# The first group's feed-forward layer in one pair of banks, eight early panels and result gathers in two bursts

## The chip, the cores and the metric

One core of a Trainium2 chip runs the whole program in one launch. The metric is the device time of one execution in microseconds (us). The engines are TensorE (PE, matrix products; its weight loads are shown apart as PEld), VectorE (DVE), ScalarE (ACT), GpSimd (POOL) and SyncE (SP). Each has an instruction stream of its own that runs in order; the streams meet by semaphores. SP and POOL issue nearly all transfers.

## The reference

Two layers over 2 sequences of 1024 tokens with 256 features, a context of 64 rows each:

```
x = x + tanh(g_xattn[0]) * attention(layernorm(x), ctx)       # one head, 64 keys
x = x + tanh(g_ffn[0])   * moe(layernorm(x))                  # 16 experts, 2 per token, + its input
x = x + tanh(g_xattn[1]) * (layernorm(x) @ W1.T + mean(ctx) @ W2.T + b)
x = x + tanh(g_ffn[1])   * ffn(layernorm(x))
moe(h): top 2 of softmax(h @ gate); y = sum_e comb_e * (silu(h @ w1_e) * (h @ w3_e)) @ w2_e
ffn(h): h = silu(h @ w1) * (h @ w2)        # 256 -> 1024, weights -1, 0, 1 with a scale per column
        h = gelu(h @ h1); h = gelu(h @ h2) # 1024 -> 1024 each
        h @ w3                             # 1024 -> 256
```

## The kernel before, in words

The 2048 tokens are 16 tiles of 128 rows and four groups of four tiles (512 tokens). Products run in fp32r, so every operand is split into a high and a low part; an expert product is three matmuls (low times high, high times low, high times high), and a product of the last layer two, since its weights are exact in the high part.

**Stage 1** (to about 65 us) is attention, routing and the expert weights' split. Tokens are sorted by expert into 47 blocks of 128 rows (`NBLK`): the first 16 blocks are the first 128 rows of each expert, the rest follow.

**Stage 2** is the loop over expert blocks, `for i in range(NBLK + DOWN)`, on each engine. POOL gathers the rows of block i (`L659`) up to six blocks ahead (`NXG`). PE turns block i + 2 (`turns`, `L1850`), together with the hidden rows of block i - 2 (`L1853`; this matmul is the mark of a turn below: the mark of block n is the turn made in iteration n - 2), runs `gate_up(i)` and then `down(i - 4)`. ACT copies the turned rows out as the high part (`high_turned`), applies silu and copies results out (`rows_out`); DVE makes the low part (`low`) and the product with the gate. SP stores the results to `ys_dram`. The results that the first group's tokens need are all in the first 16 blocks' part of `ys_dram` once those are stored, so the first group's next steps are woven into this loop at hand-written iteration numbers (`Y_AT` to `LOW4_AT`): POOL gathers the eight result tiles (`gather_rows`, `L640`), DVE adds them (`row_added`), and then, in halves of two tiles, come the statistics, the root on POOL (`root_half`, `L588`), the transposes (`turned_half`, `L1896`), high and low parts, the product with W1 (`part1_half`), the row that POOL adds (`add_row_half`, `L648`), and the same again for the LayerNorm ahead of the last layer. Iteration numbers on POOL count row gathers, which run ahead of PE's.

**Stage 3** is the feed-forward network for the four groups (`ffn(g)`), 512 tokens at a time: a first layer of eight chunks m (eight matmuls of 128 x 512 each, gate and up in one pair of banks, `L2007`, `L2010`), two layers h1 and h2 of eight chunks (16 matmuls each, `L2038`, `L2039`), and the product with w3. In the first layer, chunk m writes the pair `bank[2 * (m % 2)]` and the next, so two pairs alternate; ACT applies silu (`L1573`), DVE multiplies with the up half (`L1296`), ACT rounds the high part (`L1577`), DVE makes the low part (`L1300`).

The last layer's weights are 44 panels of 128 x 512 (`NPAN`): 0 to 7 the first layer, 8 to 23 h1, 24 to 39 h2, 40 to 43 w3. SP loads them (`load_raw`, `L375`), at most four in flight, and they are rounded in place: 0 to 7 by DVE, the others by ACT (`round_panels`, `L1531`), which counts them in `act_pan`. Panels 0 to 15 are loaded during the expert loop, 16 to 21 when the last result is stored, 22 to 43 when the first layer of the first group is through (`f_pe[FK - 1]`). What sets these times is the memory: the panels' places are used by expert weights and by the first group's buffers until then. ACT rounds five panels in the last iterations of the loop, nine in the first group's first layer and the rest in h1.

Of the kernel before, what the change touches and what calls it, by code (L numbers as in the profile page):

```python
# [25 lines left out]
ALU = mybir.AluOpType  # L26
# [25 lines left out]
NRAW = 16  # L52
# [6 lines left out]
FIRST_PAN = NRAW + (3 * 4 * 4 * 256) // (4 * 512)  # L59
# [56 lines left out]
def flamingo_kernel(nc, x, ctxT, cols, rows, wq, wkT, wvT, gate, experts, w1T, w2T, panels, consts, identity, out):  # L116
    with ExitStack() as ctx:
# [19 lines left out]
        Wr, w_end = place("Wr", [P, NPAN * PANEL], F32R)  # L137
        w_off = w_end - 4 * NPAN * PANEL
        Wraw = nc.alloc_sbuf_tensor_at("Wraw", [P, NPAN * PANEL], F32, offset=w_off)
        Ah, _ = place("Ah", [P, 4096], F32R)  # L140
        Al, _ = place("Al", [P, 4096], F32R)
        Bh, _ = place("Bh", [P, 4096], F32R)
        bl_off = at[0]
        Bl, b_end = place("Bl", [P, 4096], F32R)
# [55 lines left out]
        e_off = w_end - 4 * LATE * PANEL  # L200
# [73 lines left out]
        put = over(w_off + 4 * NRAW * PANEL, e_off)  # L274
        y_first = [put(f"y_first{r}", [P, TG, D]) for r in range(TOPK)]
        xn_first = put("xn_first", [P, TG, D])
        xTh_first, xTl_first = put("xTh_first", [P, DK, GN], F32R), put("xTl_first", [P, DK, GN], F32R)
        yb = put("yb", [P, 4, D])
# [69 lines left out]
        bank_t, bank_gu = [bank[0], bank[1], bank[4]], [bank[2], bank[3]]  # L348

        bank_y, bank_first = [bank[6], bank[5]], bank[7]  # L350
# [20 lines left out]
        def load_raw(eng, w):  # L371

            if w >= 4:
                eng.wait_ge(dma_pan[w % 4], 16 * (w // 4))
            eng.dma_start(Wraw[:, w * PANEL:(w + 1) * PANEL], panels[w]).then_inc(dma_pan[w % 4], 16)  # L375
# [7 lines left out]
        def panel(w):  # L383
            return Wr[:, w * PANEL:(w + 1) * PANEL], Wraw[:, w * PANEL:(w + 1) * PANEL]
# [9 lines left out]
        def half_turned():  # L394
            return bank_first[:, :].rearrange("p (k n) -> p k n", k=DK)
# [14 lines left out]
        def _(eng):  # L410
# [62 lines left out]
            panel_at = [PAN_AT + 3 * (w // 2) + w % 2 if w < DVE_PAN else PAN_AT + 12 + 2 * (w - DVE_PAN) for w in range(NRAW)]  # L473
            for i in range(NBLK + 2):
# [3 lines left out]
                if i == PAN_AT:  # L478
# [3 lines left out]
                    eng.wait_ge(pool_el, EL_CUT * POOL_EL)  # L482
                    eng.wait_ge(dve_el, E - POOL_EL)
                    eng.wait_ge(act_setup, ACT_LATE + 2)
                    for b in range(2):
                        eng.wait_ge(dma_xb[b], 16 * rows_stored[b])
# [54 lines left out]
        def _(eng):  # L541
# [108 lines left out]
            for i in range(NBLK):  # L650
# [13 lines left out]
                if i == Y_AT[0]:  # L664
# [11 lines left out]
                    eng.wait_ge(dve_el, E - POOL_EL)  # L676
                    for b in range(2):
                        eng.wait_ge(dma_xb[b], 16 * rows_stored[b])
                if i in Y_AT:
# [1487 lines left out]
```

## Time and profile before

| | us |
|---|---|
| timed runs | 494.70, 500.42, 785.72 |
| median of them | 500.42 |
| span of the profiled execution, first to last instruction | 514.8 |
| PE busy in it | 482.9 |
| DVE, ACT, POOL busy | 317.2, 214.0, 147.2 |

The profile is one execution, and not one of the timed runs; its own time outside the span is not listed. A busy PE is an engine with a matmul under way; matmuls overlap, so the distance between two starts tells more than the duration of one. "Idle before" in a row names what ended the wait.

### The profile page before, as it was taken

The page shows a single profiled execution, that of the slowest core. Times are in us where ns is not written, and L with a number is a line of the kernel's source. Part 1 is how long each engine was busy: PE and PEld are TensorE (multiplying, and loading weights), DVE is VectorE, ACT ScalarE, POOL GpSimd, SP SyncE. Part 2 cuts the span into 40 slices and gives each one's busy share as a digit, 9 for nine tenths or more (in the row PEclk, how much of TensorE's full clock was granted, in tenths as well). Part 3 has the DMA queues.
Part 4 walks back from the last instruction along what each step waited for, and adds up shares of the span by engine and source line. Part 5 has one row for each costly group of instructions (what it writes and reads, how often), then busy time and mean ns, then how long its engine had stood idle before and what let it go on. Part 6 is the DMA issues. An engine that isn't in the chain of part 4 may idle for free.

```text
span 514.8 us, 7849 instructions
## 1 busy us (share of the span) xinstructions
PE 482.9 (94%) x2754; PEld 414.0 (80%) x2754; DVE 317.2 (62%) x850; ACT 214.0 (42%) x444; POOL 147.2 (29%) x154
## 2 busy tenths in 40 slices
PE   8898977994889899999999999999999999999996
PEld 7787867893879678888987888897888888788886
DVE  3988855872668577548456874537677633745433
ACT  4569924671547695621254221126222133621210
POOL 1677674647562141101071110126011101000000
PEclk9989997997799999999999999999999999999999
DMA  8967432795572558422041220005032002021101
GB/s 290 339 251 245 156 93 83 211 290 167 166 220 94 177 185 268 148 81 61 22 143 43 64 78 24 1 1 163 22 102 62 1 1 81 2 77 66 42 1 47
DMA packets 34480, 58.81 MB, mean 114 GB/s; under 512 B 4545, under 2 KB 18369, under 8 KB 34370
## 3 DMA queue, kind: packets, MB, share of 16 engines
q1 hardware_dynamic: 29776, 47.12, 27.9%
q0 software_dynamic: 3840, 10.49, 7.2%
q10 hardware_dynamic: 818, 0.61, 0.4%
q8 instruction: 25, 0.41, 0.3%
q14 instruction: 21, 0.17, 0.1%
HBM read 47.85 MB, written 14.42 MB: 121 GB/s over the span
## 4 chain that ended last, share of the span: by engine, by line
PE 77%; DVE 4%; another core or an unknown queue 3%; ACT 2%; issue 2%; DMA 1%; POOLq 0%
PE bank L2038 23%; PE bank L2039 23%; PE bank L2010 6%; PE bank L2007 5%; PE bank L1613 3%; PE bank L1615 3%; PE bank L1614 3%; PE bank L2071 3%; PE bank L2070 3%; PE bank L1850 2%; PE bank L1853 1%; DVE turned L1019 1%; ACT xb L1429 1%; DMA xg_more<-xb_dram,perm 1%
## 5 line engine op out<-in xcount | busy, mean ns | idle before, releaser
L1587 ACT ACTIVATE sg<-bank,colv 128x512 f32<-128x512 f32 x64 | 44.1, 690 | 177.2 <-PE bank L2039 177.2
L2038 PE MATMUL bank<-Ah,Wr 128*128 128x512 f32 x256 | 100.3, 392 | 0.6 <-DVE sg L1296 0.6
L2038 PE MATMUL bank<-Bh,Wr 128*128 128x512 f32 x256 | 99.9, 390 | 0.0
L2039 PE MATMUL bank<-Bl,Wr 128*128 128x512 f32 x256 | 99.7, 389 | 0.0
L2039 PE MATMUL bank<-Al,Wr 128*128 128x512 f32 x256 | 99.7, 389 | 0.0
L2038 PEld LDWEIGHTS bank<-Ah,Wr 128*128 128x128 f32 x256 | 48.0, 188 | 11.9 <-DVE sg L1296 1.4
L2039 PEld LDWEIGHTS bank<-Bl,Wr 128*128 128x128 f32 x256 | 48.1, 188 | 9.8
L2038 PEld LDWEIGHTS bank<-Bh,Wr 128*128 128x128 f32 x256 | 48.1, 188 | 9.8
L2039 PEld LDWEIGHTS bank<-Al,Wr 128*128 128x128 f32 x256 | 48.1, 188 | 9.7
L1313 DVE CAST Ah<-sg 128x512 fp32r<-128x512 f32 x32 | 13.6, 426 | 60.1 <-ACT sg L1587 60.1
L1613 PE MATMUL bank<-EL,turned 128*128 (+1 forms) x133 | 42.7, 321 | 1.2 <-issue 0.9
L583 POOL TENSOR_TENSOR rstd<-veps,mhalf 128x4 f32<-128x4 f32 x6 | 8.4, 1400 | 108.8 <-DVE veps L762 61.1
L1614 PE MATMUL bank<-EH,turned 128*128 (+1 forms) x133 | 38.7, 291 | 0.0
L1615 PE MATMUL bank<-EH,turned 128*128 (+1 forms) x133 | 38.5, 290 | 0.0
L1296 DVE SCALAR_TENSOR_TENSOR sg<-bank,colv,sg 128x512 f32<-128x512 f32 x32 | 24.0, 751 | 23.1 <-ACT sg L1573 20.3
L1573 ACT ACTIVATE sg<-bank,colv 128x512 f32<-128x512 f32 x32 | 22.1, 690 | 38.4 <-PE bank L2010 35.3
L1313 DVE CAST Bh<-sg 128x512 fp32r<-128x512 f32 x32 | 13.6, 426 | 39.4 <-ACT sg L1587 39.4
L2007 PE MATMUL bank<-xTh,Wr 128*128 128x512 f32 x96 | 37.7, 392 | 0.0
L2010 PE MATMUL bank<-xTl,Wr 128*128 128x512 f32 x96 | 37.6, 392 | 0.0
L659 POOL DMA_INDIRECT xg<-xb_dram,perm x32 | 31.7, 991 | 15.5 <-PE bank L1853 6.9
L1019 DVE TENSOR_TENSOR turned<-bank,turned 128x384 fp32r<-128x384 f32 (+1 forms) x47 | 24.9, 530 | 13.6 <-ACT turned L1505 7.7
L2071 PE MATMUL bank<-Wr,Al 128*128 128x256 f32 x128 | 30.9, 283 | 0.0
(295 smaller groups left out, 1036.9 us busy)
## 6 DMA issues: line engine op xcount, KB each, us to landing
Wraw<-panels SPq DMA_DIRECT2D x44, 256.0 KB
stage<-panels SPq DMA_DIRECT2D x44, 256.0 KB
ES<-experts SPq DMA_DIRECT2D x16, 384.0 KB, 5.7
ys_dram<-yb SPq DMA_DIRECT2D x47, 128.0 KB
ys_dram<-x SPq DMA_DIRECT2D x1, 1920.0 KB, 8.8
X<-x SPq DMA_DIRECT2D x3, 512.0 KB, 7.8
xb_dram<-xb SPq DMA_DIRECT2D x3, 512.0 KB, 4.5
out<-outb SPq DMA_DIRECT2D x3, 512.0 KB
```

Source lines behind the costliest of these rows:

```text
L659: eng.indirect_dma_start(out=rows, out_offset=None, in_=xb_dram, in_offset=bass.IndirectOffsetOnAxis(ap=perm[:, i:i + 1], axis=0)).then_in ...
L1019: eng.tensor_tensor(low_[:, w], bank_t[b][:, w], high_[:, w].bitcast(F32), ALU.subtract).then_inc(b_xl, 1)
L1313: own(eng.tensor_copy(h[0][:, m, :], sg[:, r, :]))
L1587: eng.activation(sg[:, (8 * layer + m) % 3, :], bank[m % 4][:, :], ACT.Gelu, scale=colv[:, c + m:c + m + 1]).then_inc(f_act[m], 1)
L1613: mm(dst, lhs[0], rhs[1], start=first, stop=False)
L1614: mm(dst, lhs[1], rhs[0], start=False, stop=False)
L1615: return mm(dst, lhs[0], rhs[0], start=False, stop=last)
L2007: mm(dst, w[:, u, k, :], x_high[:, k, :], start=k == 0, stop=False)
L2010: ins = mm(dst, w[:, u, k, :], x_low[:, k, :], start=False, stop=k == DK - 1 and not general)
L2038: mm(bank[m % 4][:, :], Wr[:, base:base + P], h[0][:, k, :], start=k == 0, stop=False)
L2039: ins = mm(bank[m % 4][:, :], Wr[:, base:base + P], h[1][:, k, :], start=False, stop=k == FK - 1 and not general)
L2071: ins = mm(dst, hA[1][:, k, j * P:(j + 1) * P], w, start=False, stop=k == FK - 1)
```

## The change

Memory: the hidden tensors A and B of stage 3, which had places of their own, become part of one array of 76 slots of 128 x 512 (`SLOTS`), and panels are mapped to slots by `slot(w)`. Only panels 0 to 7 are loaded in the loop (`NRAW = 8`); 8 to 39 follow as soon as the last expert block's product is done, 40 to 43 when the first layer of the first group is through.

Result gathers: on POOL four follow row gather 30 and four row gather 31. The counts of stored blocks are read by four register loads in place of one instruction for all four. The half steps lie closer together (iterations 27 to 36), and each half has a bank of its own (`bank_half`); therefore from block 30 on the turns use two banks instead of three.

First layer: for the first group it moves out of `ffn` into `first_chunk`, which can be woven into the loop by `CHUNK_AT`; here that list is empty, so all eight chunks follow the last iteration. Chunks 0 to 5 and 7 use `bank[7]` and `bank[4]`, chunk 6 `bank[5]` and `bank[6]`. ACT writes silu's result to `first_gate`. ACT rounds panels 8 and 9 ahead of chunk 7 and 10 and 11 behind it, three per chunk of h1, and one per chunk of h2.

```diff
-NRAW = 16
+NRAW = 8
-FIRST_PAN = NRAW + (3 * 4 * 4 * 256) // (4 * 512)
+SLOTS = NPAN + 4096 * 4 // PANEL
+HID_A = NRAW
-Y_AT = (28, 29, 31, 32, 34, 35, 37, 38)
-ROOT2_AT, ROW_AT, ROOT3_AT = (37, 45), (38, 45), (44, 46)
-ADD_AT, STAT_AT = (25, 28, 31, 36), (26, 29, 33, 37)
-TURN3_AT, HIGH3_AT, LOW3_AT, PART_AT, X3_AT = (30, 37), (31, 38), (32, 39), (33, 40), (34, 41)
-NORM_AT, TURN4_AT, HIGH4_AT, LOW4_AT = (43, 45), (44, 47), (45, 48), (46, 48)
+Y_AT = (30, 30, 30, 30, 31, 31, 31, 31)
+ROOT2_AT, ROW_AT, ROOT3_AT = (32, 33), (32, 34), (36, 38)
+ADD_AT = (27, 28, 29, 29)
+LOW3_AT, X3_AT, NORM_AT, LOW4_AT = (29, 30), (30, 32), (33, 35), (34, 36)
+TURN3_AT, PART_AT, TURN4_AT = (29, 30), (29, 31), (34, 36)
+HIGH3_AT, HIGH4_AT = (29, 30), (34, 36)
+CHUNK_AT = ()
+RING2 = 30
-RESIDUAL_AT = (12, 13, 14, 15, 27, 30, 38, 40, 44, 47)
+RESIDUAL_AT = (12, 13, 14, 15, 24, 25, 39, 41, 43, 45)
...
+        bank_half = [bank[7], bank[4]]
+        bank_first = [[bank[5], bank[6]] if m == FK - 2 else [bank[7], bank[4]] for m in range(FK)]
+        def bank_t(n):
+            return bank[n % 2] if n >= RING2 else (bank[0], bank[1], bank[4])[n % 3]
+        def slot(w):
+            return w if w < NRAW else w + NPAN - LATE - NRAW if w < NPAN - 4 else w - NPAN + 4 + HID_A + 16
...
-            eng.wait_ge(n_T4, 2)
-            for b in range(4):
-                eng.wait_ge(dma_ys[b], 16 * len(range(b, NBLK, 4)))
             eng.wait_ge(b_y, NBLK)
             for n in range(NRAW, NPAN):
-                if n == FIRST_PAN:
+                if n == NPAN - 4:
                     eng.wait_ge(f_pe[FK - 1], 1)
...
-                    _, stored_n = nc.values_load_multi_w_load_instructions(
-                        stored[0:1, 0:4], engines=(mybir.EngineType.Pool,), min_val=16 * (E // 4),
-                        max_val=16 * (NBLK // 4 + 1), skip_runtime_bounds_check_because="DVE counts the blocks")
+                    stored_n = [eng.value_load(stored[0:1, b:b + 1], min_val=16 * (E // 4), max_val=16 * (NBLK // 4 + 1)) for b in range(4)]
...
-                if i in Y_AT:
-                    gather_rows(0, [Y_AT.index(i)])
+                gather_rows(0, [n for n in range(TOPK * TG) if Y_AT[n] == i])
...
+            def first_up(m):
+                eng.wait_ge(f_act[m], 2)
+                eng.scalar_tensor_tensor(first_gate[:, m, :], bank_first[m][1][:, :], colv[:, C_S2 + m:C_S2 + m + 1],
+                                         first_gate[:, m, :], ALU.mult, ALU.mult).then_inc(f_h[m], 1)
+            def first_low_part(m):
+                eng.wait_ge(f_hh[m], 1)
+                eng.tensor_tensor(hA[1][:, m, :], first_gate[:, m, :], hA[0][:, m, :].bitcast(F32),
+                                  ALU.subtract).then_inc(f_hl[m], 1)
+            def first_chunk(m):
+                first_up(m)
+                if m > 0:
+                    first_low_part(m - 1)
+                if len(RESIDUAL_AT) + m < NT:
+                    residual(len(RESIDUAL_AT) + m)
...
+            def first_high_part(m):
+                eng.wait_ge(f_h[m], 1)
+                if m == FK - 2:
+                    for b in range(4):
+                        eng.wait_ge(dma_ys[b], 16 * len(range(b, NBLK, 4)))
+                eng.activation(hA[0][:, m, :], first_gate[:, m, :], ACT.Copy).then_inc(f_hh[m], 1)
+            def first_chunk(m):
+                eng.wait_ge(f_pe[m], 1)
+                eng.activation(first_gate[:, m, :], bank_first[m][0][:, :], ACT.Silu,
+                               scale=colv[:, C_S1 + m:C_S1 + m + 1]).then_inc(f_act[m], 1)
+                if m > 0:
+                    first_high_part(m - 1)
...
-                if NBLK - 5 <= i < NBLK:
-                    round_panels(1)
+            for m in range(len(CHUNK_AT), FK):
+                if m == FK - 1:
+                    round_panels(2)
+                first_chunk(m)
+            first_high_part(FK - 1)
+            round_panels(2)
...
-                        if g == 0 and layer == 1:
-                            round_panels(3 if m else 2)
+                        if g == 0:
+                            round_panels(3 if layer == 1 else 1)
...
                 if n >= 3:
-                    eng.wait_ge(b_xl, n - 2)
+                    eng.wait_ge(b_xl, n - 1 if n >= RING2 + 2 else n - 2)
...
+            def first_chunk(m):
+                if m == 0:
+                    eng.wait_ge(n_l4, 2)
+                elif m == FK - 2:
+                    eng.wait_ge(b_ye, NBLK)
+                else:
+                    eng.wait_ge(f_h[m - 1 if m < FK - 1 else m - 2], 1)
+                eng.wait_ge(dve_pan, m + 1)
+                w = panel(m)[0].rearrange("p (u k n) -> p u k n", u=2, k=DK)
+                for u in range(2):
+                    for k in range(DK):
+                        dst = bank_first[m][u][:, :]
+                        mm(dst, w[:, u, k, :], xTh_first[:, k, :], start=k == 0, stop=False)
+                        ins = mm(dst, w[:, u, k, :], xTl_first[:, k, :], start=False, stop=k == DK - 1)
+                ins.then_inc(f_pe[m], 1)
+            for m in range(len(CHUNK_AT), FK):
+                first_chunk(m)
```

## Rows read from the trace of the kernel before

**Rows 1.** The page: span, and busy time, share and instructions of each engine.
```profile
span 514.8 us, 7849 instructions
PE 482.9 (94%) x2754; PEld 414.0 (80%) x2754; DVE 317.2 (62%) x850; ACT 214.0 (42%) x444; POOL 147.2 (29%) x154
```

**Rows 2.** Timeline of PE: start us, us, engine, line, tiles, count [idle before <-releaser].
```profile
108.32 0.27 PE L1853 MATMUL bank<-ident,bh 128*128 128x128 f32 x1
109.73 0.27 PE L1853 MATMUL bank<-ident,bh 128*128 128x128 f32 x1
...
117.25 0.27 PE L1853 MATMUL bank<-ident,bh 128*128 128x128 f32 x1
...
136.06 0.29 PE L1853 MATMUL bank<-ident,bh 128*128 128x128 f32 x1
...
140.89 0.27 PE L1853 MATMUL bank<-ident,bh 128*128 128x128 f32 x1
...
166.62 0.27 PE L1853 MATMUL bank<-ident,bh 128*128 128x128 f32 x1
...
169.55 0.66 PE L1896 MATMUL bank<-ident,xn_first 128*128 128x128 f32 x4 [1.12 <-DVE xTl_first L1166]
...
172.42 0.50 PE L2007 MATMUL bank<-xTh_first,Wr 128*128 128x512 f32 x1 [0.47 <-ACT yb L1519]
```

**Rows 3.** The chain that ended last, in order of time: start us, us, what.
```profile
116.97 3.12 another core or an unknown queue
...
125.61 4.50 another core or an unknown queue
```

**Rows 4.** Timeline of POOL, 110 to 143 us.
```profile
110.19 0.95 POOL L659 DMA_INDIRECT xg<-xb_dram,perm  x1 [0.98 <-PE bank L1853]
114.41 0.95 POOL L640 DMA_INDIRECT y_first<-ys_dram,slots  x1 [3.27 <-DMA ys_dram<-yb]
115.66 0.94 POOL L659 DMA_INDIRECT xg_more<-xb_dram,perm  x1 [0.30 <-issue]
...
138.38 0.72 POOL L588 TENSOR_TENSOR rstd<-veps,mhalf 128x2 f32<-128x2 f32 x1 [1.95 <-DVE veps L1161]
...
141.58 1.30 POOL L648 TENSOR_TENSOR X<-X,crow 128x512 f32<-128x512 f32 x1
```

**Rows 5.** Line 668 alone: duration in ns (min/median/max), first and last start.
```profile
L668 POOLq TENSOR_LOAD <-stored x1: 520/520/520, 110.0 to 110.0; - x1
```

**Rows 6.** The chain in order of time, at the first row gather.
```profile
65.21 2.80 DMA xg_more<-xb_dram,perm
```

**Rows 7.** Timeline of PE: a turn that waited for its row gather.
```profile
119.72 0.41 PE L1850 MATMUL bank<-ident,xg_more 128*128 128x128 f32 x2 [1.08 <-DMA xg_more<-xb_dram,perm]
```

**Rows 8.** The chain in order of time: a half's transposes, one 256-wide matmul.
```profile
137.43 0.44 PE bank L1896 x4
...
138.19 0.12 PE bank L1613
```

**Rows 9.** Timelines of ACT, DVE and PE in the first feed-forward layer.
```profile
174.55 0.69 ACT L1573 ACTIVATE sg<-bank,colv 128x512 f32<-128x512 f32 x1 [2.18 <-PE bank L2010]
175.34 0.75 DVE L1296 SCALAR_TENSOR_TENSOR sg<-bank,colv,sg 128x512 f32<-128x512 f32 x1 [3.04 <-ACT sg L1573]
187.32 0.40 PE L2038 MATMUL bank<-Ah,Wr 128*128 128x512 f32 x1
```

**Rows 10.** Stretches: us, busy of PE, PEld, DVE, ACT, POOL, granted clock, DMA, GB/s.
```profile
118.00:122.00 4.00, 2.26 (x15) 1.59 (x13) 0.29 (x1) 0.66 (x2) 2.92 (x4) 1.00 0.58 189
...
130.00:136.00 6.00, 5.20 (x24) 5.19 (x25) 3.96 (x11) 2.92 (x9) 4.30 (x5) 0.50 0.63 175
...
168.00:172.00 4.00, 2.52 (x18) 1.91 (x16) 2.39 (x7) 3.22 (x12) 0.00 (x0) 1.00 0.32 107
```

**Rows 11.** Timeline of SP behind the first feed-forward layer.
```profile
187.51 19.59 SPq L375 DMA_DIRECT2D Wraw<-panels  x22
```

**Rows 12.** Groups of instructions by line: busy us, mean ns of one.
```profile
L1531 ACT ACTIVATE Wr<-Wraw 128x512 fp32r<-128x512 f32 x36 | 21.0, 623 | 0.0
```

More of the change, by code:

```diff
@@ L134, in sem, with hidden @@
             return ctx.enter_context(nc.semaphore(name))
[L137 to L144, printed above, removed]
+        Wr, w_end = place("Wr", [P, SLOTS * PANEL], F32R)
+        w_off = w_end - 4 * SLOTS * PANEL
+        Wraw = nc.alloc_sbuf_tensor_at("Wraw", [P, SLOTS * PANEL], F32, offset=w_off)
+        def hidden(name, slot):
+            return [nc.alloc_sbuf_tensor_at(f"{name}{part}", [P, 4096], dt, offset=w_off + 4 * PANEL * (slot + 8 * n))
+                    for n, (part, dt) in enumerate((("h", F32R), ("l", F32R)))]
+        Ah, Al = hidden("A", HID_A)
+        Bh, Bl = hidden("B", SLOTS - 16)
+        first_gate = nc.alloc_sbuf_tensor_at("first_gate", [P, FK, GN], F32, offset=w_off + 4 * PANEL * (HID_A + 8))
+        bl_off, b_end = w_off + 4 * PANEL * (SLOTS - 8), w_off + 4 * PANEL * SLOTS
         X, _ = place("X", [P, NT, D])
@@ L374, in load_raw @@
                 eng.wait_ge(dma_pan[w % 4], 16 * (w // 4))
-            eng.dma_start(Wraw[:, w * PANEL:(w + 1) * PANEL], panels[w]).then_inc(dma_pan[w % 4], 16)
+            eng.dma_start(panel(w)[1], panels[w]).then_inc(dma_pan[w % 4], 16)
         rows_stored = [NG // 2, NG // 2 - 1 + 2]
@@ L383, in panel @@
         def panel(w):
[L384 removed]
+            columns = slice(slot(w) * PANEL, (slot(w) + 1) * PANEL)
+            return Wr[:, columns], Wraw[:, columns]
         def counted(g):
@@ L471, in ys_blocks @@
                 return ys_dram.rearrange("(b p) d -> b p d", p=P)[i]
-            panel_at = [PAN_AT + 3 * (w // 2) + w % 2 if w < DVE_PAN else PAN_AT + 12 + 2 * (w - DVE_PAN) for w in range(NRAW)]
+            panel_at = [PAN_AT + 3 * (w // 2) + w % 2 for w in range(NRAW)]
             for i in range(NBLK + 2):
@@ L1239, in _ @@
                         low_half(q, n_h4, n_l4)
+                for q in range(2):
+                    for j in (2 * q, 2 * q + 1):
+                        if i == ADD_AT[j]:
+                            row_added(0, j)
+                            row_statistics(0, j)
+                            if j % 2:
+                                variance_half(2, q)
+                        if i == LOW3_AT[q] and j % 2 == q:
+                            low_half(q, n_h3, n_l3)
+                    if i == X3_AT[q]:
+                        x3_half(q)
+                        statistics3_half(q)
+                if i in CHUNK_AT:
+                    first_chunk(CHUNK_AT.index(i))
+            for m in range(len(CHUNK_AT), FK):
+                first_chunk(m)
+            first_low_part(FK - 1)
             own.done()
@@ L1292, in ffn @@
                 g3 = 3 * g
-                for m in range(FK + 1):
+                for m in range(FK + 1 if g else 0):
                     if m < FK:
@@ L1301, in ffn @@
                                           ALU.subtract).then_inc(f_hl[m - 1], 1)
-                    if g == 0 and len(RESIDUAL_AT) + m < NT:
-                        residual(len(RESIDUAL_AT) + m)
                 if g == 0:
@@ L1502, in high_turned @@
             def high_turned(n):
-                b, w = n % 3, joint(n)
+                w = joint(n)
                 eng.wait_ge(b_tx, n + 1)
-                eng.activation(turned_pair(n)[0][:, w], bank_t[b][:, w], ACT.Copy).then_inc(b_xh, 1)
+                eng.activation(turned_pair(n)[0][:, w], bank_t(n)[:, w], ACT.Copy).then_inc(b_xh, 1)
             def silu(i):
@@ L1559, in _ @@
                         high_half(q, n_T4, n_h4)
-                if NBLK - 5 <= i < NBLK:
-                    round_panels(1)
+                if i in CHUNK_AT:
+                    first_chunk(CHUNK_AT.index(i))
+            for m in range(len(CHUNK_AT), FK):
[4 more added lines that the diff above has]
+            round_panels(2)
             def ffn(g, more):
                 g3 = 3 * g
-                for m in range(FK + 1):
+                for m in range(FK + 1 if g else 0):
                     if m < FK:
@@ L1944, in _ @@
                     if i == TURN4_AT[q]:
-                        if q:
-                            eng.wait_ge(n_l4, q)
                         turned_half(q, xn_first, n_xn, n_T4)
+                if i in CHUNK_AT:
+                    first_chunk(CHUNK_AT.index(i))
+            for m in range(len(CHUNK_AT), FK):
+                first_chunk(m)
             def T3(g):
@@ L1987, in low_part @@
                     return Wlo[:, w % 2, :]
-                for m in range(FK):
+                for m in range(FK if g else 0):
                     if m >= 2:
@@ L2020, in ffn @@
                         if m < 4:
-                            if layer == 1:
+                            if layer == 1 and g:
                                 eng.wait_ge(f_h[6 + m // 2], g + 1)
-                            else:
+                            elif layer == 2:
                                 eng.wait_ge(f_act[m + 4], g3 + 2 + 1)
```

84 lines of the change are left out of this document (27 added, 57 removed).

## The prediction

> **What bounds the kernel now.** I read the page first, then the chain that ended last, then the timeline of TensorE (PE), POOL, ACT and DVE in the expert stage and in the first feed-forward layer. PE is busy 94% of a span of 514.8 us [rows 1], so a change counts by the PE time that it opens or closes. Two places are not bound by PE's own work. The expert blocks should run at one block per 1.41 us (from one turn mark to the next) [rows 2], but between the turns of block 28 and of block 32 four blocks took 18.81 us instead of 5.64 [rows 2]. The chain gives 12.2 us of that to "another core or an unknown queue", in four pieces of 3.12, 1.44, 3.12 and 4.50 [rows 3]. I call these 13.2 us the hole. At the loop's end PE waits for the second half of the first group's LayerNorm chain, 1.12 us ahead of its transposes, and 0.47 us for the last output copy [rows 2]. Behind the loop PE runs matmul after matmul.
>
> **Which time the sum is made against.** The profiled execution's own run time is not listed, only its span, 514.8. Without the hole that is 501.6; the median of the timed runs is 500.42, the lowest 494.7. So the timed runs hold little of the hole, and I make the sum on the trace without it and add the difference to 500.42.
>
> **The change, part by part.**
>
> *A. The result gathers in two bursts.* Before, eight gathers lie one by one between the row gathers 28 to 38; afterwards four follow row gather 30 and four follow 31. A gather takes POOL 1.25 us start to start, and row gather 28 started at 110.19 [rows 4], so 30 starts at 112.69 and ends at 113.64. The four block-count registers now take four loads; the one load before took 520 ns [rows 5]. Three more make 1.56, and the burst starts at 115.2 (bounds: 113.9 if the loads are hidden; 117 if the wait for stored blocks, 3.27 us before [rows 4], still ends last). Then row gather 31 starts at 115.2 + 4 x 1.25 = 120.2 and row gather 32 at 126.45. A row gather lands 2.80 us after its start where it is on the chain alone [rows 6]; the one that started at 115.66 held PE until 119.72, 4.06 us, with panel loads beside it [rows 4, 7]. I take 2.80, since no panel is loaded there any more, and keep 4.06 for the range. So block 32 can be turned at 129.3. At PE's pace it was due at 117.25 + 4 x 1.41 = 122.9 [rows 2]: 6.4 us late. DVE waits in the same stretch for gathers 4 to 7 ahead of adding rows 2 and 3, and behind it in DVE's queue stands the low half of block 32, which is not there yet either; so this costs nothing twice. The first half's transposes (0.44) and its 12 products (12 x 0.12 = 1.4) [rows 8] fall into PE's wait and are paid.
>
> Next POOL does the root (0.72) and the row add (1.30) [rows 4] ahead of row gather 33, which starts at 129.7 and lands at 132.5; PE would want it at 129.3 + 1.41 + 0.44 = 131.1, so another 1.4 late. Then 1.41 for the block and 1.4 for the second half's products: block 34 at 135.3. Row gather 35 stands behind the second root and add and lands at 137.0, 0.3 late. So block 35 is turned at 137.0. Before it was at 140.89, without the hole 127.7 [rows 2]. **A costs 9.3 us by then** (6 to 13 with the bounds above; three landings are on the path).
>
> *B. From block 35 to the first layer.* Before this took 172.42 - 140.89 = 31.5 us [rows 2], with one half's transposes, both products and the LayerNorm waits in it. Afterwards two sets of transposes are left (0.9), 13 turns at 1.41 make 18.3, and the tail after the mark of block 48 is before's 172.42 - 166.62 = 5.8 without the last transposes (a wait of 1.12, then 0.44) and without the 0.47 wait: 3.8 [rows 2, 8]. Sum 23.0, so **B gives back 8.5**. With only two turn banks from block 30 on, the turn of n waits for the low half of n-2 instead of n-3; PE's products for that block wait for it right behind, so I cost it at nothing. That holds while ACT and DVE keep up with 1.41; if they do not, each block pays the lag. ACT's five panel roundings leave the loop; ACT was not last there, so nothing.
>
> *C. The first layer.* Before, its 64 products run from 172.42 to 187.32 in two pairs of banks, 14.9 us, 1.86 a chunk [rows 2, 9]. Afterwards chunks 0 to 5 and 7 share one pair, and chunk m waits until DVE has read chunk m-1. From a chunk's first product to ACT's start is 2.13, ACT takes 0.69, DVE follows 0.10 later and takes 0.75 [rows 9], and I add 0.05 back to PE: 3.72 a chunk. Five of these, then chunk 5, chunk 6 (its own banks) and chunk 7 back to back, 3 x 1.86: 24.2 us. **C costs 9.3.** ACT's and DVE's other work per chunk (rounding the high part, the low part, a residual) fits into the 3.7. PE then stands still for nearly half of this stage. In this trace the clock fell after a stretch with 2.26 us busy of 4 and stayed at 0.50, the 1.2 GHz level, through 130 to 136, but stayed at 1.00 through one with 2.52 of 4 [rows 10]; a chunk would show about 2.0 of 3.7. I take the full clock, as the products are wide.
> The Trainium skill, "TensorE: Matmul & The Clock Gate" (A second HAM failure mode: psum-queue depth-cycling), has a kernel whose PE idles briefly between groups because its PSUM banks are cycled, and whose clock swings between both levels. By that rule this stage would be dearer than by the row; that is a rival below.
>
> *D. Panels.* 32 panels now load behind the last expert block and four behind the first layer. SP issued 22 in 19.59 us, 0.89 each [rows 11]; the first that counts is rounded 22 us later, and the second layer uses two in 16 x 0.233 = 3.7 us. No wait; cover: layer C itself. ACT rounds three per chunk in the second layer and one in the third, and the 36th comes after the third layer's last activation. PE waits there for all 36 ahead of the last product: 0.1 + 0.69 + 0.62 [rows 9, 12] = **1.4 us**, which before did not exist, as all were rounded a layer earlier. SP's queue loses the panels between result stores; nobody waits for those.
>
> **Sum:** 9.3 - 8.5 + 9.3 + 1.4 = +11.5, so 500.4 + 11.5 = 511.9 us, 2.3% slower. Own range of this case: 507 to 517 (A's bounds).
>
> **Rivals.**
> 1. *The hole is half in the timed runs and the panels make it (not slower).* The hole lies at blocks 26 to 30, and SP loads panels 8 to 15 from block 20 to 34, between result stores; those eight loads leave this place. For it: the runs spread by 5.7 us (494.7 to 500.42), and the row gather of this stretch landed 1.3 us later than the one alone [rows 6, 7]. Against it: result stores and gathers stay, now in bursts. If the median holds those 5.7 us and the change frees them, the result is 494.7 + 11.5 = 506.2, 1.2% above, the same within what is measurable. It decides once about 1.5 us of such time is in the usual run. Freeing 21 us, which a gain of 2% would need, is more than the whole hole.
> 2. *The clock falls in layer C.* At 1.2 GHz a chunk's products take twice 1.86. All eight chunks low: +14.9 us; one low stretch as long as the shorter ones of the trace, about half of that. Time 519, at most 527. For: the row with 2.26 of 4. Against: the row with 2.52 of 4, and that every product is 512 columns wide. It is the mechanism of the skill's rule named above; no run here shows it in such a stage.
> 3. *The bursts are cheaper.* If the four loads run ahead of the engine and PE reaches block 31 later than I have it, A falls to 6: 508.6, 1.6% over and so within what can be told apart.
>
> **How the numbers follow.** Forecast (511.9) 0.50; rival 1 0.24; rival 2 0.13; rival 3 0.08; something unseen, either way, 0.05. The prediction is the first. The range 502 to 520 reaches over rivals 1 and 3 and the cheaper half of 2. A measurement of this kernel tells about 2% from no change, here 510.4. Slower: 0.7 of the forecast, which lies close to that line, rival 2 and a little of the rest: 0.51. Faster: a rest of rival 1, 0.05. Within 2%: 0.44.
>
> **What would show it.** In the changed kernel's trace: on POOL two runs of four result gathers with a row gather between; PE idle ahead of the turn of block 32 for 4 us or more, released by a gather; six groups of eight 512-wide products about 3.7 us apart, PE waiting for DVE between them, and two more without a gap; about 1.4 us of idle PE, released by ACT, ahead of the last product's first matmul in the first group; a loop end with no wait on the LayerNorm chain. I am wrong if the loop ends much earlier than before at equal start (then the bursts cost little or the hole was the panels'), if chunks follow at 1.9 us, or if the clock drops behind the last block.

## The result, and the profile after

The changed kernel took 509.01 us (median of 4 runs, 507.82 to 510.97); its ratio to the kernel before is 1.0251, 95% interval [1.019, 1.0311]. Run once more later, as *changed_again*, it took 508.59 beside 494.77 of the kernel before (17 runs): 1.0243 [1.0198, 1.0288]. The ratios are worked out from fast runs alone, with executions more than 1.5% above the fastest of their kernel set aside (785.72 and 501.46 of the kernel before, 501.44 of late_panels below). They are not the quotients of the medians shown, which for changed_again would be 1.028. So the change costs 10 to 14 us. That it costs time is clear; that it costs 2% is not quite, since the intervals begin at 1.019 and 1.0198. The forecast was 511.9, range 502 to 520.

The page of the changed kernel, its span and busy times; they answer to [rows 1].

```profile
span 508.8 us, 7841 instructions
PE 478.7 (94%) x2754; PEld 411.7 (81%) x2754; DVE 317.7 (62%) x850; ACT 218.6 (43%) x444; POOL 147.0 (29%) x154
```

The span is 6 us *shorter* than that of [rows 1], though the kernel is slower. The two profiled executions are not alike, and the page alone would mislead. This run took 510.97 in all, 2.2 more than its span.

PE's timeline in the changed kernel answers to [rows 2], with the marks of turns on L1896 (blocks 28, 32, 35 and the last), the first layer on L1965, h1 on L2094 and w3 on L2126.

```profile
107.98 0.27 PE L1896 MATMUL bank<-ident,bh 128*128 128x128 f32 x1
...
115.00 0.66 PE L1893 MATMUL bank<-ident,xg 128*128 128x128 f32 x2 [2.87 <-DMA xg<-xb_dram,perm]
...
119.91 0.39 PE L1656 MATMUL bank<-W1l,xTh_first 128*128 128x256 f32 x1 [1.41 <-DVE xTl_first L1170]
...
121.67 0.27 PE L1896 MATMUL bank<-ident,bh 128*128 128x128 f32 x1
...
127.87 0.39 PE L1656 MATMUL bank<-W1l,xTh_first 128*128 128x256 f32 x1 [2.61 <-DVE xTl_first L1170]
...
132.56 0.27 PE L1896 MATMUL bank<-ident,bh 128*128 128x128 f32 x1
...
154.12 0.30 PE L1896 MATMUL bank<-ident,bh 128*128 128x128 f32 x1
...
156.10 0.40 PE L1965 MATMUL bank<-xTh_first,Wr 128*128 128x512 f32 x1
...
159.67 0.50 PE L1965 MATMUL bank<-xTh_first,Wr 128*128 128x512 f32 x1 [1.56 <-DVE first_gate L1199]
...
180.88 0.47 PE L2094 MATMUL bank<-Ah,Wr 128*128 128x512 f32 x1 [0.68 <-ACT Wr L1553]
...
245.25 0.36 PE L2126 MATMUL bank<-Wr,Ah 128*128 128x256 f32 x1 [1.34 <-issue]
```

Three things stand here. The loop waits in brackets: for the row gather of block 31 (2.87) and twice for a low half made by VectorE (1.41, 2.61). The first six chunks of the first layer follow 3.6 to 3.7 apart, each but the first behind a wait of 1.56. And 1.34 us of idle stand ahead of w3. The profile names no releaser for it ("issue"); the kernel has PE wait there for ACT's count of panels, and round_four below bears that out.

POOL's timeline in the changed kernel answers to [rows 4]: result gathers on L650, row gathers on L669, the root on L598.

```profile
106.30 0.95 POOL L650 DMA_INDIRECT y_first<-ys_dram,slots  x1 [2.07 <-DMA ys_dram<-yb]
...
111.38 0.95 POOL L669 DMA_INDIRECT xg<-xb_dram,perm  x1 [0.30 <-PE bank L1896]
...
117.64 0.94 POOL L669 DMA_INDIRECT xg<-xb_dram,perm  x1 [0.30 <-issue]
...
123.94 0.72 POOL L598 TENSOR_TENSOR rstd<-veps,mhalf 128x2 f32<-128x2 f32 x1 [2.17 <-DVE veps L1165]
124.86 1.02 POOL L669 DMA_INDIRECT xg<-xb_dram,perm  x1 [0.19 <-issue]
```

The two bursts are there, 5.0 us each. The first row gather behind a burst started at 111.38 and held PE until 115.00. In the chain its landing is 3.49 (the prediction had taken 2.80), while POOL shows only 0.95. The Trainium skill, "Perfetto Trace Analysis" (DMA Instruction — SWDGE (GPSIMD)), says that such an instruction's end is the end of descriptor generation and not of the data movement; this trace agrees. The row gather of block 34 (124.86) stands behind a root that waited 2.17 for VectorE.

Stretches of the changed kernel (columns as in [rows 10]): two in the loop, two in the first layer.

```profile
114.00:119.00 5.00, 3.50 (x16) 3.28 (x16) 2.08 (x6) 1.62 (x4) 4.06 (x5) 0.66 0.43 125
...
128.00:132.00 4.00, 4.00 (x22) 4.00 (x23) 0.93 (x3) 0.49 (x1) 3.18 (x5) 0.57 0.23 66
...
156.00:163.00 7.00, 4.24 (x19) 2.85 (x17) 1.51 (x3) 2.55 (x5) 1.90 (x2) 1.00 0.81 263
163.00:181.00 18.00, 12.26 (x49) 8.78 (x50) 9.29 (x17) 7.49 (x14) 5.07 (x5) 1.00 0.90 299
```

The clock fell in the loop, behind the gaps there, and not in the first layer.

**Where the time went, by stage.** The table has differences of start times in PE's timelines, in us, so scatter of the start drops out. The column "usual before" is *before_four_loads* (below), since [rows 2] turned out to be unusual.

| stage | usual before | changed | difference | forecast |
|---|---|---|---|---|
| mark of block 28 to mark of block 35 (A) | 15.47 | 24.58 | +9.11 | +9.3 |
| mark of block 35 to the first layer (B) | 30.59 | 23.54 | -7.05 | -8.5 |
| first layer to h1 (C) | 14.91 | 24.78 | +9.87 | +9.3 |
| h1 to the end of the span (D) | 326.38 | 327.92 | +1.54 | +1.4 |
| sum | | | +13.5 | +11.5 |

Each column is one profile, and A depends on which: the seven blocks took 21.93 in the profile of changed_again and 13.64 in that of late_panels, a kernel that has A as before, so A lies between 6.5 and 10.9. B and D differ by less than 0.5 between the two profiles of the changed kernel, C by 1.8.

### The profile page after: what moved, and what is told of

Same layout as the page of the kernel before. It is cut to its first block, busy times and chain, and to the rows that moved or that the text cites. A ratio compares the mean times of both kernels' runs of the same rounds, so it can differ in the third digit from the quotient of the medians.

```text
span 508.8 us, 7841 instructions
## 1 busy us (share of the span) xinstructions
PE 478.7 (94%) x2754; PEld 411.7 (81%) x2754; DVE 317.7 (62%) x850; ACT 218.6 (43%) x444; POOL 147.0 (29%) x154
## 4 chain that ended last, share of the span: by engine, by line
PE 77%; DVE 3%; DMA 3%; ACT 2%; POOL 1%; issue 1%; POOLq 0%
PE bank L2094 23%; PE bank L2095 23%; PE bank L2063 4%; PE bank L2066 4%; PE bank L1656 3%; PE bank L1657 3%; PE bank L1658 3%; PE bank L2126 3%; PE bank L2127 3%; PE bank L1893 2%; PE bank L1965 2%; DMA xg<-xb_dram,perm 1%; PE bank L1966 1%; PE bank L1896 1%; ACT first_gate L1577 1%
## 5 line engine op out<-in xcount | busy, mean ns | idle before, releaser
L1630 ACT ACTIVATE sg<-bank,colv 128x512 f32<-128x512 f32 x64 | 44.1, 690 | 172.0 <-PE bank L2095 172.0
L2094 PE MATMUL bank<-Ah,Wr 128*128 128x512 f32 x256 | 100.1, 391 | 0.7 <-ACT Wr L1553 0.7
L2094 PE MATMUL bank<-Bh,Wr 128*128 128x512 f32 x256 | 99.9, 390 | 0.0
L2094 PEld LDWEIGHTS bank<-Ah,Wr 128*128 128x128 f32 x256 | 48.1, 188 | 11.8 <-issue 1.1
L2094 PEld LDWEIGHTS bank<-Bh,Wr 128*128 128x128 f32 x256 | 48.1, 188 | 9.8
L1338 DVE CAST Ah<-sg 128x512 fp32r<-128x512 f32 x32 | 13.6, 426 | 59.6 <-ACT sg L1630 59.6
L1338 DVE CAST Bh<-sg 128x512 fp32r<-128x512 f32 x32 | 13.6, 426 | 39.7 <-ACT sg L1630 39.7
L669 POOL DMA_INDIRECT xg<-xb_dram,perm x32 | 31.4, 981 | 9.3 <-issue 7.4
L2126 PE MATMUL bank<-Wr,Ah 128*128 128x256 f32 x128 | 30.9, 283 | 1.3 <-issue 1.3
L1618 ACT ACTIVATE sg<-bank,colv 128x512 f32<-128x512 f32 x24 | 16.5, 689 | 35.5 <-PE bank L2066 35.5
L1023 DVE TENSOR_TENSOR turned<-bank,turned 128x384 fp32r<-128x384 f32 (+1 forms) x47 | 24.7, 526 | 10.5 <-ACT turned L1530 10.3
```

Source lines behind the costliest of these rows:

```text
L669: eng.indirect_dma_start(out=rows, out_offset=None, in_=xb_dram, in_offset=bass.IndirectOffsetOnAxis(ap=perm[:, i:i + 1], axis=0)).then_in ...
L1338: own(eng.tensor_copy(h[0][:, m, :], sg[:, r, :]))
L1630: eng.activation(sg[:, (8 * layer + m) % 3, :], bank[m % 4][:, :], ACT.Gelu, scale=colv[:, c + m:c + m + 1]).then_inc(f_act[m], 1)
L2094: mm(bank[m % 4][:, :], Wr[:, base:base + P], h[0][:, k, :], start=k == 0, stop=False)
L2126: mm(dst, hA[0][:, k, j * P:(j + 1) * P], w, start=k == 0, stop=False)
```

## The experiments

Each was timed against the kernel before in five rounds; the first four shared their runs of it (median 495.53 of 23), the next four too (494.77 of 17), and the last four (495.58 of 29).

**two_pairs: C alone undone.**

```diff
-bank_first = [[bank[5], bank[6]] if m == FK - 2 else [bank[7], bank[4]] for m in range(FK)]
+bank_first = [[bank[5], bank[6]] if m % 2 else [bank[7], bank[4]] for m in range(FK)]
...
-                elif m == FK - 2:
+                elif m == 1:
...
-                    eng.wait_ge(f_h[m - 1 if m < FK - 1 else m - 2], 1)
+                    eng.wait_ge(f_h[m - 2], 1)
```

> The changed kernel (509.0 us) with only the banks of its first layer altered: odd chunks use a second pair, so chunk m waits for chunk m-2. By the prediction's term C the stage takes 14.9 us again in place of 24.8 (first product of the first layer to first product of h1), and the time falls by 9.3 us to about 499.7. Rival: the stage is then held by something the waits had covered, the loads and roundings of the late panels or the last stores, and less than half comes back: above 504. If the clock had fallen in the stage with the gaps, more than 10 would come back; the trace shows 1.00 there, so I expect no more.

Measured: 498.95, ratio 1.0059 [1.0029, 1.009]. PE's timeline of two_pairs, first product of the first layer and of h1:

```profile
151.18 0.40 PE L1965 MATMUL bank<-xTh_first,Wr 128*128 128x512 f32 x1
...
166.75 0.47 PE L2094 MATMUL bank<-Ah,Wr 128*128 128x512 f32 x1 [0.69 <-ACT Wr L1553]
```

The stage takes 15.57. That is 14.9 and the 0.69 for which h1 waits until ACT has rounded its first panels; the changed kernel has that wait too (0.68). So the single pair costs 24.78 - 15.57 = 9.2 us, and nothing took the place of the bank waits. The run times fell by 9.6 to 10.1.

**half_order: PE's and VectorE's order around the low halves.**

```diff
-LOW3_AT, X3_AT, NORM_AT, LOW4_AT = (29, 30), (30, 32), (33, 35), (34, 36)
-TURN3_AT, PART_AT, TURN4_AT = (29, 30), (29, 31), (34, 36)
+LOW3_AT, X3_AT, NORM_AT, LOW4_AT = (29, 30), (31, 32), (33, 35), (34, 36)
+TURN3_AT, PART_AT, TURN4_AT = (29, 30), (30, 32), (34, 36)
```

> The changed kernel with two places in the hand-written order altered: the W1 product of each half stands one iteration later on TensorE, and VectorE makes the first half's residual sum and statistics one iteration later, so behind the second half's low part. In the changed kernel's trace TensorE waited 1.41 and 2.61 us for these low parts. Theory 'order': these 4.0 us are a loss of their own that the prediction had put at nothing, and 3 to 4 of them go: 505 to 506. Rival 'POOL queue' (the prediction's step A): the gathers of blocks 32 and 34 set the pace and the wait only changes its name: 508 to 509.

Measured: 507.16, ratio 1.0205 [1.0158, 1.0251]; 1.4 us less than changed_again, with overlapping intervals. The waits in PE's timeline of half_order:

```profile
114.48 0.41 PE L1893 MATMUL bank<-ident,xg 128*128 128x128 f32 x2 [2.87 <-DMA xg<-xb_dram,perm]
...
120.18 0.41 PE L1893 MATMUL bank<-ident,xg 128*128 128x128 f32 x2 [2.47 <-DMA xg<-xb_dram,perm]
...
127.36 0.41 PE L1893 MATMUL bank<-ident,xg 128*128 128x128 f32 x2 [2.31 <-DMA xg<-xb_dram,perm]
```

Both waits for VectorE are gone, and waits of nearly the same length for the row gathers of blocks 32 and 34 stand in their place. So the rival named here was mostly right: the gathers set the pace. But the chain of half_order reaches the last of them through VectorE, whose adds of rows 2 and 3 and statistics the root on POOL waits for:

```profile
119.07 1.30 DVE X L1150
...
123.42 0.72 POOL rstd L598
...
124.33 2.89 DMA xg<-xb_dram,perm
```

**order_and_root: the same, and the second root behind the next row gather.**

```diff
-ROOT2_AT, ROW_AT, ROOT3_AT = (32, 33), (32, 34), (36, 38)
+ROOT2_AT, ROW_AT, ROOT3_AT = (32, 34), (32, 35), (36, 38)
```

> As half_order (507.2), and on POOL the root of the second half one row gather later (behind that of block 34) and the row add of that half one later still. In half_order's trace TensorE waits 2.31 us for the gather of block 34, which stands on POOL behind a root that waits 2.1 us for VectorE. Theory 'a waiting root blocks the row gather': that wait shrinks and 1.5 to 2.3 us go, to 505 to 505.7. Theory 'POOL has too much to do in all': the gather of block 35 is late by as much instead, and the time stays at 507.

Measured: 507.19, ratio 1.0229 [1.0185, 1.0273], no better than half_order. The wait for block 34's row gather went, but its timeline has 3.19 ahead of block 32 in place of 2.47, and 0.50 of clock in 115 to 120. From block 28 to 35 it took 22.39, from there to the first layer 24.96 (half_order: 24.45 and 23.19). One profile each cannot tell which of these ate the gain; the times say only that there is none.

**spread_gathers: A and B undone together.**

```diff
-Y_AT = (30, 30, 30, 30, 31, 31, 31, 31)
+Y_AT = (28, 29, 31, 32, 34, 35, 37, 38)
...
```

All half steps got the numbers of the kernel before as well.

> The changed kernel with the eight result gathers one by one and all half steps at the iteration numbers of the kernel before; memory, panels, banks and first layer as changed. It undoes A and B together. By the prediction's sum (A +9.3, B -8.5) it gains 0.8: about 508. By the rows of the changed kernel's trace (A +14.7 from the mark of block 28 to that of block 35, B -8.0) it gains 6.7: about 502.3. If the stalls of the kernel before come from the one-by-one gathers themselves, it gains less and the times scatter by 5 us or more.

Measured: 505.87, ratio 1.0206 [1.0151, 1.0261]; 3.1 less than the first median of the changed kernel, 2.7 less than changed_again. From block 28 to the first layer its trace shows 45.25, the changed kernel's 48.12. So A and B together cost about 3 us by this run, whose interval overlaps that of changed_again: more than the 0.8 of the prediction, less than the 6.7 that I had read by setting the changed trace against a pace of 1.41 a block. The usual run does not have that pace here. The third theory, times that scatter by 5 us, is not settled: five of the six runs lie between 505.62 and 507.84, one at 510.98.

**late_panels: the kernel before without panel loads 8 to 15 in the loop.**

```diff
-                if NBLK - 5 <= i < NBLK:
-                    round_panels(1)
...
-            for n in range(NRAW, NPAN):
+            for n in range(EARLY, NPAN):
```

EARLY is 8, in SP's list of loads in the loop too; the counts are read by four loads, and ACT rounds four panels per chunk in h1 in place of three.

> The kernel before (median 499.5, lowest 494.7) with panels 8 to 15 not loaded during the loop but with the next ones behind it, ScalarE's five roundings in the loop moved behind it, and the block counts read by four loads. Rival 1 of the prediction (those loads make the stalls): the median comes down to 494.5 to 496.5 and the times lie close together. The forecast's assumption (the usual run holds none of it): the median stays within 1.5 us of the kernel before in the same rounds. Third: the stalls come without these loads too (the trace of before has one at 71 to 80 us, ahead of them): median and scatter stay.

Measured: 495.31, ratio 0.9987 [0.9961, 1.0013]; times from 493.95 to 498.26 and one of 501.44, beside 493.26 to 499.77 and one of 501.46. Neither the median nor the upper end moved by more than the noise. Rival 1 of the prediction falls as far as a usual run goes: these loads cost it nothing. The long stalls themselves stand in the profile of the kernel before alone. The one at 75 to 80 us comes ahead of SP's first panel load in that trace (97.61); whether the loads had a part in the later one no run shows.

**changed_again: the changed kernel, as a base.**

> The changed kernel once more, as the base of this set of runs. Expected 507.8 to 511 as before; against the kernel before, whose median over 23 runs was 495.5, that is a ratio of 1.025 to 1.029. If the ratio of 1.025 rested on a high median of four runs of the kernel before, the new one lies above it.

Measured: 508.59, ratio 1.0243 [1.0198, 1.0288]; the ratio did not rise. Its profile differs from the first above all in where the clock fell. Stretches of changed_again:

```profile
110.00:122.00 12.00, 7.14 (x58) 6.56 (x57) 9.57 (x23) 4.22 (x11) 9.97 (x10) 1.00 0.49 142
122.00:130.00 8.00, 5.57 (x47) 5.16 (x46) 5.85 (x17) 3.24 (x9) 6.52 (x8) 1.00 0.33 100
...
157.00:163.00 6.00, 4.06 (x10) 2.75 (x11) 1.94 (x5) 1.21 (x2) 1.89 (x2) 0.72 0.95 294
```

Here the clock held in the loop and fell in the first layer. Blocks 28 to 35 took 21.93 (24.58 in the first profile), and the first layer 26.55 (24.78). PE had waited 1.89 for VectorE just ahead of it (the other waits of the stage are 1.56). At 0.72 of the clock 6 us lose up to 1.7, which is about that difference.

**round_four: D alone undone.**

```diff
-                            round_panels(3 if layer == 1 else 1)
+                            round_panels(4 if layer == 1 else 0)
```

> The changed kernel, with ScalarE rounding four panels per chunk of h1 and none in h2 (before this: three and one). By term D of the prediction the wait of 1.34 us ahead of the first group's last product goes, 1.3 less than the base of this set. Rival: ScalarE, with 0.69 + 4 x 0.62 = 3.2 us of work per chunk of 3.73, runs late in h1, and nothing is won.

Measured: 506.73, ratio 1.0222 [1.0172, 1.0273]; 1.9 less than the base, with overlapping intervals. The trace is sharper: from h1 to the end it takes 326.49, the changed kernel 327.92, and no wait stands ahead of w3. So D is 1.4.

**before_four_loads: a usual run of the kernel before.** Its only edit is four register loads in place of one instruction.

```diff
-                    _, stored_n = nc.values_load_multi_w_load_instructions(
...
+                    stored_n = [eng.value_load(stored[0:1, b:b + 1], min_val=16 * (E // 4), max_val=16 * (NBLK // 4 + 1)) for b in range(4)]
```

> The kernel before with the block counts read by four register loads in place of one, nothing else. Its profile is to show the expert loop in a usual run. If the stall of 13.2 us in the profile of before was of that one execution, the marks of blocks 28 to 35 lie about 13.6 us apart, as with late_panels, in place of 23.64, and the time is that of the kernel before within 0.5%. If the loads cost on POOL's path what A put on them, it is 0.5 to 1.6 slower.

Measured: 495.64, ratio 1.001 [0.9977, 1.0042]. The loads cost nothing that shows. PE's timeline (marks of blocks 28, 32 and 35 on L1851, first layer on L2005, h1 on L2036):

```profile
105.65 0.27 PE L1851 MATMUL bank<-ident,bh 128*128 128x128 f32 x1
...
108.84 0.41 PE L1848 MATMUL bank<-ident,xg_more 128*128 128x128 f32 x2 [1.85 <-DMA xg_more<-xb_dram,perm]
...
114.70 0.27 PE L1851 MATMUL bank<-ident,bh 128*128 128x128 f32 x1
...
121.12 0.27 PE L1851 MATMUL bank<-ident,bh 128*128 128x128 f32 x1
...
123.93 0.39 PE L1611 MATMUL bank<-W1l,xTh_first 128*128 128x256 f32 x1 [1.35 <-DVE xTl_first L1164]
...
151.71 0.50 PE L2005 MATMUL bank<-xTh_first,Wr 128*128 128x512 f32 x1 [0.47 <-ACT yb L1517]
...
166.62 0.40 PE L2036 MATMUL bank<-Ah,Wr 128*128 128x512 f32 x1
```

The seven blocks take 15.47 here (13.64 in late_panels), not 23.64 as in [rows 2]. But they don't take 9.87 (7 x 1.41) either, nor the 10.4 that the prediction had left without the hole (127.7 - 117.25): a usual run waits in this stretch as well, for gathers above all.

**pairs_spread_round, pairs_order_round and earlier_halves: several parts at once.** The first has the edits of two_pairs, spread_gathers and round_four, the second those of two_pairs, order_and_root and round_four, the third those of the first with other numbers:

```diff
-Y_AT = (28, 29, 31, 32, 34, 35, 37, 38)
-ROOT2_AT, ROW_AT, ROOT3_AT = (37, 45), (38, 45), (44, 46)
+Y_AT = (30, 30, 31, 32, 33, 34, 35, 36)
+ROOT2_AT, ROW_AT, ROOT3_AT = (36, 40), (37, 40), (41, 44)
...
```

> Three undone at once: two bank pairs (as two_pairs), gathers and half steps at the numbers of the kernel before (as spread_gathers), four roundings per chunk of h1 (as round_four). What stays of the change is the memory, the late panels and the four loads. If the three parts add up (-10.0, -3.1, -1.9 in their medians against 509), it comes to 494 to 495, the kernel before within 0.5%. If the late panels or the memory cost something of their own, it stays above 497.

> The bursts kept: two bank pairs, the order and root of order_and_root, four roundings per chunk. Sum of the medians: 507.2 - 10.0 - 1.6 = 495.6, ratio 1.00 to 1.005. It tells whether the bursts themselves, with their waits mended where that was possible, still cost against the one-by-one gathers of pairs_spread_round: 1 us more than that by the sum.

> As pairs_spread_round, but the gathers start two row gathers later (30, 30, 31 to 36) and the half steps behind them lie closer, so that the second half is through some four iterations before the loop ends. Theory: POOL's wait for the first 16 stores (2.36 us in the trace of before_four_loads) and TensorE's wait of 1.11 us at the loop's end go, 1 to 2 us less than pairs_spread_round: 493 to 494, at best 0.5% below the kernel before. Rival: POOL's work in all bounds this stretch, and nothing is won.

Measured: 497.54, ratio 1.0017 [0.9978, 1.0055]; 497.4, ratio 1.003 [0.9999, 1.006]; 494.45, ratio 0.9964 [0.9926, 1.0002]. With A, B, C and D undone the changed kernel is the kernel before, so the new memory and the late panels cost nothing that can be told apart in the times (the wait of 0.7 ahead of h1 stays in the three traces). The first two medians lie 2 to 3 above the sums that I expected. With C and D undone, bursts or spread gathers make no difference either: block 28 to the first layer takes 48.15 with the spread ones and 46.86 with the bursts. With 45.25 in spread_gathers and 45.44 in changed_again that is scatter as large as the effect, so all that the runs bear out of A and B together is a cost of 0 to 3 us. earlier_halves is the best version, but its gain of 0.36% is not certain. In its trace the wait at the loop's end is gone, and block 28 to the first layer takes 44.39 (46.06 in before_four_loads).

**woven_chunks: six chunks between the expert blocks, with the single pair.**

```diff
-CHUNK_AT = ()
+CHUNK_AT = (38, 39, 40, 41, 42, 43)
```

> The changed kernel with its first six chunks of the first layer between the expert blocks (iterations 38 to 43) and the same single bank pair. If C is only the idle time between a chunk's products and VectorE's reading of the bank, a block's products cover it: the loop grows by 6 x 1.86 = 11.2 us and the stage behind it shrinks from 24.8 to about 3.7, but then h1 comes too early for panels 8 and 9, which are loaded only when the last block is done (about 6 us until they are rounded). Sum about -8: 500 to 502. Rival: the panels' wait eats more (every panel up to 23 late): 504 or above.

Measured: 508.57, ratio 1.0235 [1.0188, 1.0281]: nothing gained. PE's timeline of woven_chunks, marks of two blocks with chunks between them, and later h2:

```profile
141.59 0.27 PE L1896 MATMUL bank<-ident,bh 128*128 128x128 f32 x1
...
143.09 0.50 PE L1965 MATMUL bank<-xTh_first,Wr 128*128 128x512 f32 x1 [0.17 <-DVE first_gate L1199]
...
145.26 0.27 PE L1896 MATMUL bank<-ident,bh 128*128 128x128 f32 x1
...
208.82 0.79 PE L2094 MATMUL bank<-Bh,Wr 128*128 128x512 f32 x1 [3.08 <-DVE Bl L1340]
```

DVE's timeline of woven_chunks, ahead of that:

```profile
207.00 0.69 DVE L1315 SCALAR_TENSOR_TENSOR stage<-stage,Wr 128x512 f32<-128x512 f32 x1 [10.24 <-DMA stage<-panels]
```

In the loop it went as theory C says: a block and a chunk take 3.67 together (1.41 and 1.86 make 3.27), the block covers the bank's turnaround, and PE waits only 0.17. From block 35 to h1 it took 42.90, the changed kernel 48.32, so 5.4 were won. Then both theories missed the place where it was lost. From h1 to the end it took 334.99 in place of 327.92. SP issues the loads for DVE's check of the panels behind all the panel loads; DVE waited 10.24 for the first of them, and the low part that PE needs stood behind that check in DVE's queue. PE waited 3.08 and then 0.46, and behind the wait its granted clock was 0.58 and 0.57 from 208 to 216 us, which loses up to 3.4 more; together that is the 7.07. The changed kernel's DVE does not wait for these loads: there SP begins the panels 23 us ahead of h1 (157.74), here 4.6 (168.26).

## Why the prediction was right, point by point

**The kernel is slower, and C carries it.** C and D cost what the prediction gave them, for the reasons it gave; A's price came out by other reasons. C was put at 9.3 and measured 9.9 in the trace, of which 9.2 are the single pair (two_pairs). The chain of the changed kernel has the cycle as the prediction built it: ACT 0.70, DVE 0.76, then PE.

```profile
161.84 0.70 ACT first_gate L1577
162.57 0.76 DVE first_gate L1199
163.37 0.50 PE bank L1965
```

The rest of C is the 0.68 for which h1 waits until ACT has rounded its first panels, where the prediction's D said "no wait". The wait that D did name was put at 1.4 and measured 1.34 as a wait and 1.4 by round_four. B was put at 23.0 us from block 35 on and measured 23.54; the usual run needs 30.59 there, not 31.5, so it gives back 7.0.

**A had two errors that nearly cancel.** The prediction said that without the hole block 35 is turned 10.4 after block 28; a usual run takes 13.6 to 15.5. And it said that the first half's transposes and products "fall into PE's wait and are paid". They don't: in PE's queue they stand ahead of the next turn, and waited themselves for VectorE's low halves. The 1.41 is the way of the transposes through ACT and VectorE; in the 2.61 VectorE had the second half's adds and the first half's statistics ahead. So the sign that was named, 4 us of idle ahead of block 32's turn, is not there: 2.87 stand ahead of block 31's and none ahead of block 32's. The mark of block 35 came 24.58 and 21.93 after that of block 28 in two profiles, 19.75 had been forecast. By half_order PE's waits for the low halves were not the price by themselves, since the gathers behind them were late by nearly as much. Both ways lead over VectorE, whose work here the prediction had put at nothing ("so this costs nothing twice"). In the changed kernel's chain all the work between these lines is VectorE's:

```profile
119.17 0.69 DVE xTl_first L1170
...
127.22 0.60 DVE xTl_first L1170
127.87 0.39 PE bank L1656
```

In half_order it is VectorE, then POOL's root and a gather. No run makes VectorE's part smaller, so how much of the extra is VectorE and how much POOL's queue stays open; order_and_root moved the root out of the way and won nothing. In the first profile the slow clock is part of it too (21.93 and 24.58 differ by 2.65).

**The starting point was wrong by five.** I took 501.6, the span without the hole, as equal to the median of 500.42. The median of 17 to 29 runs is 494.8 to 495.6, and the 500.42 was a high draw: of the 69 later runs of the kernel before three took longer. That the trace seemed to agree with it has two reasons. The hole was too long in my reading: a usual run takes 9.05 from block 28 to 32 (105.65 to 114.70; 7.08 in late_panels) and not 5.64, so the excess was 9.8 to 11.7, not 13.2. And that trace holds a second stall which I had not looked for, in the first blocks. The chain of the kernel before, in order of time:

```profile
75.59 1.12 another core or an unknown queue
...
77.11 2.44 another core or an unknown queue
```

The mark of block 10 lies at 90.18 there, at 79.64 in before_four_loads. So the profiled execution was over 20 us longer than a usual one (spans of 514.8 and 493.0), in more places than one. Not all of that is standing still: in and behind the stalls the granted clock was low (0.51 and 0.64 from 78 to 86 us, 0.50 to 0.74 from 122 to 138), which makes at most 10 of the 21.8. A sum of +11.5 on a start of 500.4 gave 511.9; +13.5 on 495.5 gives 509.0. That the number came within 3 us is partly luck: the start was five too high and the sum two too low.

**The rivals.** Rival 1 (the panels make the hole, and the usual run holds half of it) is refuted by late_panels for the usual run. What causes the stalls stays open: the chains of the 13 other profiles have no such piece, with the panel loads (before_four_loads) or without. Rival 2 (the clock falls in layer C) named a real mechanism in the wrong place and size: with the single pair the stage ran at 24.7 to 24.9 in five profiles and at 26.55 in one, where the clock was 0.72 for 6 us. The clock that swings between both levels, as the Trainium skill, "TensorE: Matmul & The Clock Gate" (A second HAM failure mode: psum-queue depth-cycling), has it for a kernel with such gaps, shows in that one profile of six and not in the other five. That the width of the products holds the clock, as the prediction argued, no run shows. In the loop the gaps cost clock more often, with bursts or without: over 4 us somewhere between 110 and 132 it was below 0.7 in the first profile, half_order, order_and_root, spread_gathers, round_four, late_panels, woven_chunks, pairs_spread_round and pairs_order_round, and it was 1.00 throughout in changed_again, two_pairs, before_four_loads and earlier_halves. Rival 3 (A falls to 6, a time of 508.6) can't be told from the forecast by these runs: A was 9.1 with the first profile of the changed kernel and 6.5 with the second, and the four loads cost nothing that shows, as that rival supposed.

## What to carry to other kernels

Take the cost of a stretch from a usual run with its usual waits, not from the best pace seen elsewhere in the trace; when one profile is longer than the runs, count all its stalls before setting one of them equal to the difference. Work that stands ahead of a blocked instruction in the same queue is not hidden by that instruction's wait: it adds its own waits first. A stage with gaps, like the first layer here, may cover transfers and checks of the next one: closing its gaps where it stood brought all of them back (two_pairs), moving its work ahead of the loads brought nothing (woven_chunks).

## What I had not expected of the hardware

The same program's profiles differ by where TensorE's clock falls: 0.66 and 0.57 in two stretches of the loop in one execution, 1.00 there and 0.72 in the first layer in the next, with spans of 508.8 and 508.0. The times of the kernel before scatter upwards, with panel loads 8 to 15 in the loop or without, and they go with that clock: of its 69 runs in the experiments, the 47 with a mean granted clock of 0.995 or more took 493.3 to 497.8 (median 494.9), the 19 with 0.992 or less took 496.2 to 501.5 (median 498.9). So much of the scatter is how often the clock fell in an execution; what decides that, the runs don't show.
